# The output bias folded into the value rows, and the second expert's first weight matrix loaded during the stage before

## The reference

```python
q = jnp.broadcast_to(slot_query, (Bx, NS, D))            # NS = 16 slots
o = q + _mha(q, x, x, d_Wq, ..., d_Wo, d_bo)             # dispatch: slots read the tokens
h = _layernorm(os, e_ln_g, e_ln_b)                       # one slot per expert
u = silu(einsum('besd,edf->besf', h, e_W1) + e_b1)       # e_W1: 16 x 512 x 2048
g = silu(einsum('besd,edf->besf', h, e_Wg) + e_bg)
y = einsum('besf,efd->besd', u * g, e_W2) + e_b2
o = o + y
out = _mha(x, o, o, c_Wq, ..., c_Wo, c_bo)               # combine: tokens read the slots
x = x + out
```

## Time and profile before

| | |
|---|---|
| median of 3 runs | 3295.51 us (3294.92 to 3296.34) |
| the profiled execution | 3303.09 us, span 3301.3 us |
| TensorE matmul busy | 2990.0 us, 91% of the span |
| VectorE busy | 1859.6 us, 56% |
| ScalarE busy | 1063.0 us, 32% |
| GpSimd busy | 943.3 us, 29% |
| moved by DMA | 438.54 MB, mean 133 GB/s |
| dispatch, experts, combine start about at | 2577, 2682, 3171 us |

### The profile page before, as it was taken

One profiled execution on the slowest core, in us unless ns is written; L12 is line 12 of the kernel. 1 busy time (PEld: TensorE's weight loads), 2 busy tenths in 40 slices (PEclk: granted clock), 3 DMA queues, 4 the chain that ended last, 5 costly groups with the idle time before them and its releaser, 6 DMA issues. The chain is left out here.

```text
span 3301.3 us, 54795 instructions
## 1 busy us (share of the span) xinstructions
PE 2990.0 (91%) x19242; PEld 1673.0 (51%) x19242; DVE 1859.6 (56%) x2220; ACT 1063.0 (32%) x2510; POOL 943.3 (29%) x606
## 2 busy tenths in 40 slices
PE   8998799999999999999999789999999787777778
PEld 6876333333333333333333678888888343333335
DVE  4355878787887878787883345555554510000038
ACT  3222344444444444444444223333333100101123
POOL 0000554445444444445454022222222000000013
PEclk9999899999999999999999889999999888878889
DMA  4453512121212212131200411111111669999954
GB/s 166 178 204 128 128 49 62 51 70 44 70 53 55 69 48 60 52 73 43 69 16 4 150 42 64 64 64 64 64 64 65 243 249 420 420 421 420 421 226 162
DMA packets 181219, 438.54 MB, mean 133 GB/s; under 512 B 17470, under 2 KB 51928, under 8 KB 156457
## 3 DMA queue, kind: packets, MB, share of 16 engines
q1 hardware_dynamic: 174057, 425.19, 36.8%
q10 hardware_dynamic: 6976, 10.75, 0.9%
HBM read 351.74 MB, written 83.89 MB: 132 GB/s over the span
## 5 line engine op out<-in xcount | busy, mean ns | idle before, releaser
L785 ACT ACTIVATE B_e<-B_pS 128x512 f32<-128x512 f32 (+3 forms) x1280 | 619.2, 534 | 850.0 <-PE B_pS L865 427.9
L640 POOL TENSOR_TENSOR B_em<-B_e,B_mask 128x1024 f32<-128x1024 f32 (+1 forms) x320 | 670.9, 2098 | 730.7 <-ACT B_e L785 693.9
L703 DVE TENSOR_REDUCE mx<-B_pM 128x4 f32<-128x2048 f32 (+2 forms) x299 | 588.9, 1969 | 38.7 <-PE B_pM L847 20.3
L865 PE MATMUL B_pS<-B_qs,B_ks 128*128 128x512 f32 (+3 forms) x1280 | 505.2, 447 | 43.4 <-issue 19.7
L696 DVE SCALAR_TENSOR_TENSOR B_em<-B_mask,B_e 128x1024 f32<-128x1024 f32 (+1 forms) x320 | 354.4, 1108 | 257.9 <-PE B_pN L895 256.3
L865 PEld LDWEIGHTS B_pS<-B_qs,B_ks 128*128 128x128 f32 x1280 | 227.8, 192 | 363.1 <-issue 238.5
L883 PE MATMUL B_pD<-B_e,B_tiny 128*32 128x512 f32 (+3 forms) x2560 | 310.0, 557 | 0.0
L889 PE MATMUL B_pD<-B_em,B_ones 128*32 128x512 f32 (+3 forms) x2560 | 301.2, 543 | 0.3 <-DVE B_em L696 0.3
L895 PE MATMUL B_pN<-B_em,B_v 128*32 128x512 f32 (+3 forms) x2560 | 293.4, 530 | 0.0
L2089 PE MATMUL E_pI<-ring,hT 128*32 128x512 f32 x1024 | 184.5, 815 | 101.1 <-DMA ring<-in_L_ffn_e_W_dram 57.8
L2012 DVE TENSOR_TENSOR E_ug<-E_pT,bT 128x32 f32 x32 | 5.7, 192 | 445.2 <-PE E_pT L2099 445.2
(11 more groups left out here) (288 smaller groups left out, 4764.2 us busy)
## 6 DMA issues: line engine op xcount, KB each, us to landing
ring<-in_L_ffn_e_W_dram SPq DMA_DIRECT2D x128, 1024.0 KB, 21.8
ring<-in_L_ffn_e_Wg_dram SPq DMA_DIRECT2D x64, 1024.0 KB, 23.6
B_qs<-q_hi SPq DMA_DIRECT2D x64, 256.0 KB, 4.5
B_ks<-k_hi SPq DMA_DIRECT2D x64, 256.0 KB, 3.9
E_xq<-xT_sc ACTq DMA_DIRECT2D x18, 512.0 KB, 10.3
ring<-x_sc SPq DMA_DIRECT2D x36, 256.0 KB, 2.6
qc<-in_x_dram SPq DMA_DIRECT2D x34, 256.0 KB, 2.7
qc<-a_sc SPq DMA_DIRECT2D x34, 256.0 KB, 3.0
```

The source lines that it names most:

```text
L640: nc.gpsimd.tensor_tensor(em[:, f % SLOTS_EM, DVE_HEADS:, w0:], e[:, f % SLOTS_E, DVE_HEADS:, w0:], mask[:, DVE_HEADS:, u0:u0 + BLK - w0], ...
L703: nc.vector.tensor_reduce(mx[:, :, qt, c], pM[:, :, 0:w], AX.X, ALU.max).then_inc(max_taken, 1)
L785: nc.scalar.activation(e[:, f % SLOTS_E, h, w0:], pS[:, h % SBANKS, w0:], ACT.Exp, scale=SCALE).then_inc(exp_ready, 1)
L865: last = nc.tensor.matmul(pS[:, h % SBANKS, w0:], ks[:, kb // NT, h, kb % NT * P:(kb % NT + 1) * P], qs[:, qb, h, w0:], start=True, stop=( ...
```

## The change

Three edits. In dispatch the first expert's pieces are issued differently: six at once behind the weights of the stage, and one behind each later chunk. In addition the second expert's W1 (4 pieces) is loaded in this stage, into `second`, the upper half of the columns of `qc`: three pieces when all chunks are mixed and the sums of the weights are taken, the fourth when the product `out` is made (the places hold scores, tokens and Wo until then). In experts the second expert's W1 product reads `second`; the ring places of W1 are refilled with the third expert's W1 instead. In combine the addition on GpSimd is gone; a one-row matmul (`share`, 64 columns of 1/16, times `bo`) starts each accumulation of `vo`, so that each value row has a sixteenth of the bias, and VectorE waits for the x tile itself.

```diff
+def load_second(eng, second, loaded, W1, pieces):
+
+    for k in pieces:
+        eng.dma_start(second[:, k, :], W1[1, k * P:(k + 1) * P, :]).then_inc(loaded, 16)
...
             sp.dma_start(wo[:, :, :], Wo.rearrange("(k p) n -> p k n", p=P)).then_inc(weights_loaded, 16)
+            ahead = PIECES - (CHUNKS - 2)
+            load_expert(sp, ring, piece_loaded, 0, W1, Wg, W2, range(ahead))
             for n in range(2, CHUNKS):
                 sp.wait_ge(mixed, n - 1)
                 tokens(n)
-                load_expert(sp, ring, piece_loaded, 0, W1, Wg, W2, range(2 * (n - 2), 2 * (n - 1)))
+                load_expert(sp, ring, piece_loaded, 0, W1, Wg, W2, [ahead + n - 2])
+            sp.wait_ge(mixed, CHUNKS)
+            sp.wait_ge(total_ready, B)
+            load_second(sp, second, second_loaded, W1, range(KD - 1))
+            sp.wait_ge(made, nth["out"] + 1)
+            load_second(sp, second, second_loaded, W1, [KD - 1])
...
             sp.dma_start(rows[:, :][NS:R, :], b2).then_inc(small_loaded, 16)
-            with sp.Fori(1, NS) as e:
-                sp.wait_ge(inner_made, 2 * e - 1)
-                carry(sp, sp_carried)
-                load_expert(sp, ring, piece_loaded, e, W1, Wg, W2, range(0, KD))
+            def refill(e, first):
+
+                if first is not None:
+                    sp.wait_ge(inner_made, 2 * e - 1)
+                    carry(sp, sp_carried)
+                    load_expert(sp, ring, piece_loaded, first, W1, Wg, W2, range(0, KD))
                 sp.wait_ge(inner_made, 2 * e)
                 carry(sp, sp_carried)
                 load_expert(sp, ring, piece_loaded, e, W1, Wg, W2, range(KD, 2 * KD))
                 sp.wait_ge(y_done, e)
                 carry(sp, sp_carried)
                 load_expert(sp, ring, piece_loaded, e, W1, Wg, W2, range(2 * KD, PIECES))
+
+            refill(1, 2)
+            refill(2, None)
+            with sp.Fori(3, NS) as e:
+                refill(e, e)
             weights, tiles, bo, bias = combine_room(ring)
...
-            with pe.Fori(0, NS // 2) as i:
+            def inner_products(e, n):
+
+                at_least(pe, inner_taken, 2 * e)
+                apart = n == 0 and isinstance(e, int) and e == 1
+                if apart:
+                    pe.wait_ge(second_loaded, 16 * KD)
+                for k in range(KD):
+                    piece = second[:, k, :] if apart else ring[:, n * KD + k, :]
+                    if not apart:
+                        pe.wait_ge(piece_loaded[n * KD + k], 16 * (e + (n == 1 or (isinstance(e, int) and e == 0))))
+                    for c in range(CF):
+                        last = nc.tensor.matmul(pI[c * R:(c + 1) * R, n, :], hT[:, k, :], piece[:, c * BLK:(c + 1) * BLK],
+                                                start=(k == 0), stop=(k == KD - 1), tile_position=(0, c * R))
+                last.then_inc(inner_made, 1)
+
+            def pair(i):
                 for u in range(2):
                     e = 2 * i + u
                     for n in range(2):
-                        pe.wait_ge(inner_taken, 2 * e)
-                        for k in range(KD):
-                            pe.wait_ge(piece_loaded[n * KD + k], 16 * (e + 1))
-                            for c in range(CF):
-                                last = nc.tensor.matmul(pI[c * R:(c + 1) * R, n, :], hT[:, k, :], ring[:, n * KD + k, c * BLK:(c + 1) * BLK],
-                                                        start=(k == 0), stop=(k == KD - 1), tile_position=(0, c * R))
-                        last.then_inc(inner_made, 1)
+                        inner_products(e, n)
...
-                    pe.wait_ge(ug_ready, e)
+                    at_least(pe, ug_ready, e)
...
                     last.then_inc(y_done, 1)
+
+            pair(0)
+            with pe.Fori(1, NS // 2) as i:
+                pair(i)
...
             pool.memset(bd[:, :, :, :, :, :], 0.0).then_inc(zeroed, 1)
-            pool.wait_ge(operands_loaded, TAKEN)
-
-            def tick(i, j, valid):
-                n = NT * i + j
-                if valid(n):
-                    pool.wait_ge(tile_loaded[j], 16 * (i + 1))
-                    nc.gpsimd.tensor_tensor(x2[:, j, :], x2[:, j, :], bo, ALU.add).then_inc(xb_ready, 1)
-
-            ticks(pool, tick)
+            pool.memset(share[:, :], 1.0 / H).then_inc(share_ready, 1)
...
                     dve.wait_ge(out_ready, c + 1)
-                    dve.wait_ge(xb_ready, c + 1)
+                    dve.wait_ge(tile_loaded[(j + NT - LAG_C) % NT], 16 * (i + (j >= LAG_C)))
...
             pe.wait_ge(bd_ready, 1)
+            pe.wait_ge(share_ready, 1)
             for b, banks in enumerate((pO, pS)):
                 for g in range(HG):
                     r = g % 2 * HPG * RT
+                    nc.tensor.matmul(banks[r:r + HPG * RT, g // 2, :], share[:, :], bo[0:1, :], start=True, stop=False,
+                                     tile_position=(0, r))
                     last = nc.tensor.matmul(banks[r:r + HPG * RT, g // 2, :], bd[:, 1, b, g, :, :].rearrange("p h s -> p (h s)"),
-                                            wo[:, g, :], start=True, stop=True, tile_position=(0, r))
+                                            wo[:, g, :], start=False, stop=True, tile_position=(0, r))
...
             piece_loaded = [nc.alloc_semaphore(f"piece_loaded{n}") for n in range(PIECES)]
+            second, second_loaded = qc[:, :, B * T // 2:], nc.alloc_semaphore("second_loaded")
```

More of the change, by code:

```diff
@@ L1626, in load_expert, with dispatch @@
         eng.dma_start(dst, src).then_inc(loaded[n], 16)
-def dispatch(nc, sem, s_sc, dqb, spare, xn_sc, slot_query, Wv, bv, Wo, bo, ln_g, ln_b, b1, bg, W1, Wg, W2, ring, piece_loaded, o, hT, bT):
+def load_second(eng, second, loaded, W1, pieces):
+    for k in pieces:
+        eng.dma_start(second[:, k, :], W1[1, k * P:(k + 1) * P, :]).then_inc(loaded, 16)
+def dispatch(nc, sem, s_sc, dqb, spare, xn_sc, slot_query, Wv, bv, Wo, bo, ln_g, ln_b, b1, bg, W1, Wg, W2, ring, piece_loaded, second, second_loaded, o, hT, bT):
     with ExitStack() as ctx:
@@ L1914, in combine_room, with experts @@
     return weights, tiles, bo, bias
-def experts(nc, sem, W1, Wg, W2, b2, xT_sc, c_Wq, c_bq, ring, piece_loaded, o, hT, bT, qc, o2, c_Wk, c_bk, c_Wv, c_bv, c_Wo, c_bo,
+def experts(nc, sem, W1, Wg, W2, b2, xT_sc, c_Wq, c_bq, ring, piece_loaded, second, second_loaded, o, hT, bT, qc, o2, c_Wk, c_bk, c_Wv, c_bv, c_Wo, c_bo,
             x2_sc, operands_loaded, tile_loaded):
@@ L2072, in queries @@
             def queries(u, e, g):
-                pe.wait_ge(q_taken, 2 * e)
+                at_least(pe, q_taken, 2 * e)
                 for mm in range(2):
@@ L2140, in combine @@
         fold = sb("F_fold", [P, 2, R], F32)
+        share = sb("F_share", [1, HPG * RT], F32)
         bd = sb("F_bd", [P, 2, B, HG, HPG, RT], F32)
@@ L2169, in combine @@
         q_staged = sem("F_q_staged")
-        xb_ready = sem("F_xb_ready")
+        share_ready = sem("F_share_ready")
         score_ready = sem("F_score_ready")
@@ L2441, in decoder_layer @@
                      ffn("e_ln_g"), ffn("e_ln_b"), ffn("e_b1"), ffn("e_bg"), ffn("e_W1"), ffn("e_Wg"), ffn("e_W2"),
-                     ring, piece_loaded, o, hT, bT)
+                     ring, piece_loaded, second, second_loaded, o, hT, bT)
             phase(experts, ffn("e_W1"), ffn("e_Wg"), ffn("e_W2"), ffn("e_b2"), xT_sc, ffn("c_Wq"), ffn("c_bq"),
-                    ring, piece_loaded, o, hT, bT, qc, o2, ffn("c_Wk"), ffn("c_bk"), ffn("c_Wv"), ffn("c_bv"), ffn("c_Wo"), ffn("c_bo"),
+                    ring, piece_loaded, second, second_loaded, o, hT, bT, qc, o2, ffn("c_Wk"), ffn("c_bk"), ffn("c_Wv"), ffn("c_bv"), ffn("c_Wo"), ffn("c_bo"),
                     x2_sc, operands_loaded, tile_loaded)
```

## The result

The changed kernel takes **3303.94 us** (median of 13 runs, 3297.05 to 3307.46), the kernel before 3295.5 (13 runs beside them, 3289.1 to 3300.05): a ratio of 1.0024, interval 1.0015 to 1.0033. It is slower by 8 us, and the forecast of 3280.2 was wrong in sign. Run again beside other experiments it stood at 1.0012 (1.0002 to 1.0022). The profiled execution took 3305.96 us, span 3304.2 (before: 3301.3).

A forecast was written before the change was run, and what follows sets the result against it. Bounds taken: DMA in experts, TensorE in dispatch when tokens come in time, VectorE and TensorE nearly full in combine. -10.0 - 3.1 - 6.5 + 4.3 = -15.3 from 3295.5 gave 3280.2 us, range 3276 to 3287.

The forecast's parts named there:

- The step that failed: Start of combine: eight added bias matmuls cost like their 128-row neighbours, column halves overlapping, +4.3 us (bounds +1.5 and +9.9).
- (a): Start of combine: matmuls keep strict order, only every second pair overlaps, 6.9 us instead of 4.3, total 3282.8; 13%.
- (b): Start of combine: the half clock lasts through the added matmuls, +9.9 us instead of 4.3, total 3285.8; 9%.
- (g): Experts: refills come later and the queue runs dry for a moment in every expert, slower, 3310 at 2 us each; 3%.
- (c): After combine's start: with more matmuls before it the clock may stay up, saving some 2.5 us, total 3277.5; 12%.
- (d): Combine's loop: held by the way from `sc` over ScalarE to `probT`, 1 us gained instead of 6.5, 3285.7; 6%.
- (f): Experts: W1 ahead brings nothing, the saving is waited for again where the order joins the old one, 3290.2; 4%.
- (e): Dispatch: the third chunk waits 3 us for its tokens, total 3282.6; 3%.
- Over 12 us for the 16 matmuls: Start of combine: a sign named for a wrong forecast; the right one was 9.7 us to ScalarE's second copy.
- W1 ahead, -10.0: Experts: four W1 pieces leave the DMA-bound stage at 2.49 us each, 10.0 us less (bounds 8 and 10.4).
- Six pieces ahead, -3.1: Dispatch: the last four chunks' waits go, 3.75 us, minus a new 0.6 us wait: 3.1 us less (bounds 1.5 and 3.7).
- Combine's loop, -6.5: Combine's loop: VectorE loses its 0.7 us stall, 27 ticks of 2.90 plus six branches of 0.4, 6.5 us less.

The follow-up runs named there:

- share over 128 rows: The changed kernel with the bias matmul over 128 rows (weights 1/2048) instead of one row, same order: 3284.47 us, 0.9953 of the kernel before.
- one row, grouped: The changed kernel with the four one-row matmuls of each bank pair issued together ahead of its four products: 3285.21 us, 0.9956 of the kernel before.
- before again: The kernel before, unchanged, measured and profiled once more as its own control: 3297.79 us, ratio 0.9995.
- the change again: The changed kernel, unaltered, measured and profiled once more on the same chip: 3305.64 us, 1.0012 of the kernel before.
- Loads only: The kernel before with only the edits of dispatch and experts, combine as before: 3290.86 us, 0.9973 of the kernel before.
- fold only: The kernel before with only combine's edit (one-row bias matmuls, no GpSimd addition), dispatch and experts as before: 3312.84 us, 1.0043 of the kernel before.

## Why the prediction was wrong, step by step

**The step that failed** is "The pairs now go one after the other on the same 64 columns of the array, and the two halves overlap with an offset of about two: 18 steps instead of 8, 10 x 0.43 = +4.3 us", and ahead of it "I cost it like its neighbours of 128, which stream as many columns". The term measured +24.7 us. The experiments part it in three, each the difference of two traces:

- eight more matmuls that overlap, with the clock rising as before: 8.7 - 5.4 = +3.3 us (share over 128 rows). The forecast's own mechanism, and nearly its number; the halves even overlapped without an offset.
- the clock stays at half: 14.5 - 8.7 = +5.8 us (one row, grouped), of which some 0.6 us are the three changes of rows between the groups, 0.2 us each. One trace of each version; the times don't show it.
- no overlap between neighbours of 1 and 128 rows: 30.1 - 14.5 = +15.6 us (the change against grouped); some 2 us of it are the twelve further changes of rows.

One row streams as many columns as 128, and that part of the cost was right; what I did not see was that it also changes what may run beside it. No row of before could show it, since all its neighbours there have 128 rows. The upper bound of +9.9, "18 steps, all at half", was made of overlapping steps and left out the dearest case: 16 matmuls one after the other at half clock. By the earlier trace rows one of an overlapping pair costs 0.85 us there, so alone it is 2 x 0.85, and sixteen are 27 us. An unknown operation needed that bound, and even it falls short of 30.1: one alone took 1.90 us, 0.2 more than its two passes.

**The rivals.** (a), strict order, didn't happen as I meant it: with 128 rows the second half's share ran beside the first's across the product between them, 8.7 us where strict order gave 5.4 + 6.9 = 12.3. The Trainium skill (TensorE: Matmul & The Clock Gate, Part 3, The mechanism) says that matmuls start and end strictly in order; the two halves of this trace do not, and the measurement decides. (b), the half clock, did happen, but was priced for overlapping matmuls. (g), the one slower rival, named the wrong place: the queue didn't run dry, the DMA share is 1.02. (c) didn't happen: the clock was lower for longer, not up. (d) and (f) didn't either: the loop gave back 9.5 us and the stage with W1 ahead 10.2. (e) came in part, below. "Over 12 us for the 16 matmuls" was the sign named for an error, and it is the row that shows it.

**W1 ahead, -10.0.** Right: from the end of the mixing to combine's first matmuls 2658.15 to 3173.43 is 515.3 us before and 2656.04 to 3161.13 is 505.1 after, -10.2; against before again (2653.40 to 3166.97) -8.5. The nine traces with the new loads have 504.8 us on average, the three with the old ones 514.3: -9.5.

**Six pieces ahead, -3.1.** Right in kind, but too large. TensorE's timeline in dispatch, idle time in brackets:

```profile
2605.15 8.83 PE L1849 MATMUL D_pU<-qc 128*128 128x512 f32 x16
2614.74 41.47 PE L1849 MATMUL D_pU<-qc 128*128 128x512 f32 x96 [0.76 <-DMA qc<-xn_sc]
2656.04 0.95 PE L1883 MATMUL D_bank<-D_ones,D_total 128*128 128x1 f32 x8
```

The new wait is 0.76 us (forecast 0.6) and the four later ones are gone. From first load to the end of the mixing it takes 77.8 us, against 80.7 and, again, 79.6: -1.8 to -2.9. That pair was lucky. In the other traces of the same order the new wait is anything from 0.19 to 2.41 us, here in the change again and in the grouped version:

```profile
2613.87 34.80 PE L1849 MATMUL D_pU<-qc 128*128 128x512 f32 x80 [0.19 <-DMA qc<-xn_sc]
2608.10 43.13 PE L1849 MATMUL D_pU<-qc 128*128 128x512 f32 x96 [2.41 <-DMA qc<-xn_sc]
```

The nine with the new order take 77.5 to 80.0 us to the end of the mixing, 78.6 on average; the three with the old one 78.9 to 80.7, 79.7 on average. So some 1.1 us were gained, less than the scatter. And SP's queue:

```profile
2656.24 17.44 SPq L1632 DMA_DIRECT2D qc<-in_L_ffn_e_W_dram  x4
2688.96 2.09 SPq L1626 DMA_DIRECT2D ring<-in_L_ffn_e_W_dram  x4
```

three loads at 2656 us and the fourth 17 us later, before the stage's own first load: hidden, as forecast. Loads only came to -8.9 us in time (interval -12.2 to -5.9), a little under the 13.1.

**Combine's loop, -6.5.** The mechanism was right, the size too small: -9.5 us. The 0.4 us at the branch, six times, was not there: the earlier trace rows shows a wait of 0.23 us, not 0.4, and now the tick is 2.88 us on average with the branches in it, and the loop keeps TensorE busy 99% of the time. That the stall hung on GpSimd's addition is shown by the two halves: from 3213 to 3285 us `prob` takes 1146 ns on average in loads only, which keeps the addition, and 425 in fold only.

**The sum.** With +24.7 in the place of +4.3 and -9.5 in that of -6.5, my sum becomes -10.0 - 3.1 - 9.5 + 24.7 = +2.1 us, 3297.6. With the average over all traces for the loads, -10.6 in the place of -13.1, it becomes +4.6. The change measured +8.4 by the medians (+7.9 by the ratio) and, again, +4.0 by the ratio (+0.7 to +7.3; +6.3 by the medians). So the terms explain the sign and at least half of the size; up to 4 us beyond them, in the first comparison, lie ahead of dispatch or in scatter, and stay open.

## What to carry to other kernels

A constant folded into a matmul was cheap here only where the added matmuls ran side by side with their neighbours: give a rank-one term all 128 rows (weights divided by 128, the operand already stands in all partitions), which cost 3.3 us here instead of 24.7, or leave it to the copy out of PSUM, which cost 0.2 a copy. When an operation is added that the trace doesn't hold, the upper bound of its price is "nothing beside it, at the low clock" (27 us here for the 16, against 30.1 measured), not the neighbour's price. And a gain and a loss in one change should be timed apart: here 8.9 us of gain and 14.2 of loss lay under a result of 4 to 8.

## What the runs showed of the hardware

- Column halves of TensorE work side by side when neighbours have the same number of rows, 1 or 128 (3.67 and 3.61 us for four at half clock): with 128 rows throughout, at half clock a pass on both halves takes 0.86 us (3168.76 to 3169.62), so a pair of matmuls of two passes each some 1.72 us. With 1 or 64 rows between neighbours of 128 each matmul of 512 columns takes 1.90 us alone, at half clock; with 65 rows they overlap again (30.1, 30.5 and 10.2 us for the 16). That up to 64 rows the matmul claims a part of the array and above it the whole is how I read it; the records don't name it, and neighbours that both have 64 rows were not tried.
- With 128 rows throughout, a matmul on the other half is not held up by one queued before it for the first half (four records of two shares from 3167.86 on, the first product at 3169.62).
- The granted clock stayed at 0.51 for 30 us with TensorE busy 29.75 of them, and at 0.50 with 13.80 of 14 where four one-row matmuls alternated with four full ones; with 128 rows it was 1.00 from 3172 us on, 4 us after the first. In the four traces that alternate 1 or 64 rows with 128 it never rose within the 30 us.
- VectorE's product beside GpSimd's addition: the stall of 0.7 us a tick went with the addition, all of it (mean 1120 ns before, 424 after).
